# Expert products on gathered tokens: 23 tiles of one expert for two batches in place of 16 products for each batch

## The chip, the core and the metric

One core of one Trainium2 chip runs the whole program. The metric is the device time of one execution in microseconds (us). The engines are TensorE (PE; its weight loads stand as PEld), VectorE (DVE), ScalarE (ACT), GpSimd (POOL) and SyncE (SP, which only issues transfers). Each runs its own queue in order and waits on semaphores for the others.

## The reference

The input x has 8 batches of 512 tokens with 256 features. After a layer norm, two layers read the same normed x and both are added to x: a state-space layer (input product, 4-tap convolution, a linear recurrence, silu, output product), and attention with 16 heads plus a mixture of experts. The change touches the mixture only:

```python
gate = softmax(xn @ W_gate + b_gate)             # 8 experts
top_g, top_i = top_k(gate, 2)
combine = sum(one_hot(top_i, 8) * top_g[..., None], axis=2)
expert_out = einsum("bsd,edf->bsef", xn, W_experts) + b_experts
moe_out = einsum("bsef,bse->bsf", expert_out, combine)
out = x + state_space(xn) + attention(xn) + moe_out
```

Only two of the eight experts have a weight other than zero for a token.

## The kernel before

The program is a loop over steps, 256 of them and a tail of 16. Step t makes the scores of one block of queries for two heads on PE (`score`, tile SB), their row maximum on DVE (`largest`, mx, line 942), and, 11 steps behind, the turned scores (`turned`, TB), the exponentials on ACT (Pt, line 732) and the products with V (`values`). Eight steps are one group of heads, 32 steps one batch. SP copies the split q and k of a group into place (`half_stack`, 12 transfers each 8 steps) and the maxima (`max_row`).

Everything else is cut into units that a planner (`plan`) puts into the steps as PE has time by a table of costs: T (transposes of xn), V, Q (products), Z and Y (state space), O (its output product), C (transposed gate weights), P (attention turned back), X (maxima), and M, the expert products. A batch has 16 M units: i = 4 * (pair of experts) + (block of 128 tokens). Each is six matmuls of 512 columns, since every product is made of high and low halves (`three`, line 393): 128 tokens by two experts, for all tokens and all experts. ACT copies each half out of the bank times its gate weight into one of four buffers mt (line 595), POOL adds mt into acc, the output tile of the batch (`grow`, line 996). SP stores acc when all is in it (`store`) and loads x of a later batch into the same buffer.

The gates of a batch are computed in 22 small instructions on DVE, POOL and ACT (`gate`, tiles G, g4, cpad, cst). POOL besides that makes the low halves xl (line 1100) and yl (line 1108), which the Z and O units wait for, and adds attention (line 1005). At the start POOL also turns a kernel row into a matrix by three transfers that wait for each other (kd, rd, Rraw, lines 1080 to 1085); unit G of step 2 (line 485) waits for the last.

Of the kernel before, what the change touches and what calls it, by code (L numbers as in the profile page):

```python
# [7 lines left out]
F32R = mybir.dt.float32r  # L8
ALU = mybir.AluOpType
# [9 lines left out]
NM = 4  # L19
# [4 lines left out]

Unit = namedtuple("Unit", "kind b i t read bank use frees item before")

COST = {"T": 0.45, "V": 0.75, "Q": 1.42, "Z": 2.05, "Y": 1.42, "C": 0.45, "M": 1.42, "O": 1.5, "G": 2.8, "B": 0.55,
        "X": 0.15, "P": 0.45}

WANTED = {("T", i): -30 for i in range(2)}  # L30
WANTED.update({("V", i): -30 for i in range(4)})
WANTED.update({("Z", i): -20 for i in range(2)})
WANTED.update({("Q", i): -30 for i in range(4)})
WANTED.update({("Y", i): 4 * i - 8 for i in range(4)})
WANTED.update({("M", i): 2 * i for i in range(16)})
# [4 lines left out]
def plan():  # L40
# [6 lines left out]
    todo = [(k, b, i) for b in range(NB) for k, i in WANTED if b == 0 or k not in "GB"]  # L47
# [5 lines left out]
    def soonest(kind, b, i):  # L53

        if kind == "T":
            return max([ln.get(b, END) + 5, 7] + [after(("M", b - 2, n), 1) for n in range(16) if b >= 2])
# [10 lines left out]
        if kind == "Y":  # L67
            t = after(("Z", b, 1), 1) if i == 0 else after(("Y", b, i - 1), 4)
            return max(t, after(("B", 0, 3), 1)) if b == 0 else t
        if kind in "CM":  # L70
            return after(("V", b, 3), 8 if kind == "M" else 9)
# [7 lines left out]
    last, spent = STEPS + LAG - 3, 0.0  # L79
    for t in range(END):  # L80
        row = steps[t]
        left = sum(COST[u[0]] for u in todo) + sum(fixed(n) + (COST["X"] + COST["P"]) / 8 for n in range(t, last))
        spent = min(spent, 0.0) + left / max(last - t, 1) - fixed(t)
# [23 lines left out]
    for b in range(NB):  # L107
# [3 lines left out]
        assert b < 2 or at["M", b - 2, 15] < at["V", b, 3] + 6  # L111
# [4 lines left out]
    for t, row in steps.items():  # L116
        units[t] = []
        for k, (kind, b, i) in enumerate(row):
# [4 lines left out]
            frees[bank] += kind not in "MO"  # L123
# [5 lines left out]
            item += 2 * (kind in "MO")  # L129
# [16 lines left out]
ON = {name: on for name, on, _ in GATE}  # L146

# [19 lines left out]
def store_at(b):  # L167

    return max(UNIT["P", b, 4 * b + 3].read + 1, UNIT["M", b, 15].read + 2, UNIT["O", b, 3].read + 2)
# [13 lines left out]
def program(nc, x, wqk, bqk, wvg, bv, bg, win, bin_, cw, cwt, cb, A, AT_, Bp, Cp, Dp, wout, bout, wexp, bexp, out, kd, rd):  # L183
    ctx = ExitStack()
    with ctx:
# [18 lines left out]
        uc = sb("uc", [128, 2, 512])  # L204
# [6 lines left out]
        xTh1 = sb("xTh1", [128, 2, 512], F32R)  # L211
        xTl1 = sb("xTl1", [128, 2, 512], F32R)
        yh = sb("yh", [128, 4, 512], F32R)
        yl = sb("yl", [128, 4, 512], F32R)
        xTh = [sb("xTh0", [128, 2, 512], F32R), xTh1]
        xTl = [sb("xTl0", [128, 2, 512], F32R), xTl1]
# [43 lines left out]
        G = sb("G", [128, 6, 4, 8])  # L260
        g4 = sb("g4", [128, 6, 4])
        cpc = sb("cpc", [16, 1])
# [32 lines left out]
        s_out = sem("stored")  # L295
# [8 lines left out]
        s_ex, s_mh, s_ot = sem("exp_done"), sem("max_hi"), sem("ot_copied")  # L304
        s_xTh, s_V, s_qkh, s_zh = sem("xT_hi"), sem("V_copied"), sem("qk_hi"), sem("z_hi")
# [7 lines left out]
        s_cv, s_y, s_rc = sem("conv_taps"), sem("y_done"), sem("recip_done")  # L313
        s_kv, s_kp, s_Rl = sem("krylov_copied"), sem("kernel_row"), sem("R_lo")
        s_bw, s_bl = sem("bias_products"), sem("b_lo")

        s_id, s_pc, s_pad, s_rs = sem("identity"), sem("pool_consts"), sem("pads"), sem("rstd_done")
# [5 lines left out]
        def kp_rows(w):  # L323
# [10 lines left out]
            (uc[:, :, :].rearrange("p a c -> p (a c)").rearrange("p (k n) -> p k n", k=4), wout, wouth[:, :, :], woutl[:, :, :], 0.5),  # L334
# [19 lines left out]
        def bank_read(u):  # L354
            return (s_mc, u.item + 2) if u.kind in "MO" else (s_free[u.bank], u.frees)
# [9 lines left out]

        def x_loaded(b):
            return s_x[b % 3], 16 * (b // 3 if b % 3 == 0 else b // 3 + 1)

        def half_stack(e, g, h, s):

            r, p = g % 3, 64 * (g % 2) + 32 * h
# [857 lines left out]
```

## Time and profile before

| | |
|---|---|
| time, median of 3 runs | 831.44 us (830.02 to 836.89) |
| profiled execution, its own time | 838.47 us |
| its span, first to last instruction | 836.7 us |
| PE busy | 783.3 us, 94% |
| DVE busy | 579.1 us, 69% |
| ACT busy | 528.9 us, 63% |
| POOL busy | 380.3 us, 45% |

Busy time of PE is modelled and its matmuls overlap, so what a unit costs is read from the starts of its matmuls. Waiting, branching, register and transfer-issuing instructions are not in the busy times. A releaser after an idle time is inferred from the semaphores.

### The profile page before, as it was taken

Reading aid. Unit: us, or ns where it says so; the run is one execution under the profiler, and the core shown is the slowest. Engines: PE = TensorE matmul, PEld = TensorE weight load, DVE = VectorE, ACT = ScalarE, POOL = GpSimd, SP = SyncE. Lnnn points to the kernel's source line nnn. Section 1 sums busy time; section 2 is a strip of 40 time slices with the busy share of each in tenths; the row PEclk is TensorE's granted clock in tenths of the full one; section 3 lists DMA queues with packets and bytes.
Section 4 is the critical chain, followed back from the end, with each engine's and each line's share of the span. In section 5 each row is a group of like instructions: output and inputs, shape, how many; then the busy total and the mean of one; then the engine's idle time right before and its main releaser. Section 6 shows DMA issues by size and latency. Waiting matters only on the chain.

```text
span 836.7 us, 13124 instructions
## 1 busy us (share of the span) xinstructions
PE 783.3 (94%) x4366; PEld 449.9 (54%) x4366; DVE 579.1 (69%) x834; ACT 528.9 (63%) x916; POOL 380.3 (45%) x524
## 2 busy tenths in 40 slices
PE   7579998989999999999999999999899999999996
PEld 5445564545554555556555465555465555555552
DVE  4466885796648885688857877768866698557820
ACT  3324765667566775677756676667756677566674
POOL 4433463346253363524733527443454336354583
PEclk9868999999999999999999999999999999999997
DMA  5700111112011311112111311113101121112000
GB/s 191 179 8 17 26 39 39 40 38 74 17 43 36 89 39 39 40 39 81 32 34 29 83 38 39 40 39 90 40 19 39 30 57 38 40 40 64 2 2 26
DMA packets 32387, 39.69 MB, mean 47 GB/s; under 512 B 8433, under 2 KB 18455, under 8 KB 32320
## 3 DMA queue, kind: packets, MB, share of 16 engines
q1 hardware_dynamic: 31262, 36.94, 17.3%
q0 software_dynamic: 384, 1.12, 0.5%
q10 hardware_dynamic: 674, 0.80, 0.3%
q8 instruction: 35, 0.57, 0.3%
q14 instruction: 32, 0.26, 0.1%
HBM read 8.90 MB, written 4.59 MB: 16 GB/s over the span
## 4 chain that ended last, share of the span: by engine, by line
PE 70%; DVE 18%; issue 6%; POOL 2%; ACT 1%; DMA 1%; ACTq 0%; SPq 0%; POOLq 0%; DVEq 0%
PE PS L393 36%; PE SB L518 11%; DVE mx L942 9%; PE PS L548 9%; PE TB L532 5%; PE PS L443 4%; DVE ys L798 3%; PE PS L409 1%; DVE ys L794 1%; POOL acc L996 1%; PE PS L490 1%; PE PS L405 1%; DVE th L968 1%; DVE xl L830 1%; DMA kst<-qkh 1%
## 5 line engine op out<-in xcount | busy, mean ns | idle before, releaser
L942 DVE TENSOR_REDUCE mx<-SB 128x2 f32<-128x1024 f32 x256 | 312.9, 1222 | 188.0 <-PE SB L518 187.3
L996 POOL TENSOR_TENSOR acc<-acc,mt 128x256 f32<-128x256 f32 x320 | 248.3, 782 | 233.2 <-ACT mt L595 177.8
L732 ACT ACTIVATE Pt<-TB 128x1024 f32<-128x1024 f32 x256 | 262.8, 1027 | 33.5 <-PE TB L532 31.0
L595 ACT ACTIVATE mt<-PS,cpad 128x256 f32<-128x256 f32 x256 | 107.4, 471 | 93.7 <-PE PS L393 93.2
L518 PE MATMUL SB<-kst,qst 48*128 48x512 f32 x512 | 130.0, 504 | 26.2 <-DVE mx L942 19.4
L548 PE MATMUL PS<-Pt,V 128*17 128x512 f32 x1024 | 136.0, 603 | 1.1 <-ACT Pt L732 1.1
L518 PEld LDWEIGHTS SB<-kst,qst 48*128 48x128 f32 x512 | 48.3, 186 | 133.0 <-DVE mx L942 69.8
L393 PE MATMUL PS<-weh,xTh 128*128 128x512 f32 x256 | 112.9, 441 | 2.7 <-DVE ml L806 1.2
L532 PE MATMUL TB<-qst,kst 50*128 50x512 f32 x512 | 104.4, 403 | 1.6 <-ACT Pt L732 1.4
L393 PE MATMUL PS<-wel,xTh 128*128 128x512 f32 x256 | 101.8, 398 | 0.0
L393 PE MATMUL PS<-weh,xTl 128*128 128x512 f32 x256 | 101.4, 396 | 0.0
L798 DVE SCALAR_TENSOR_TENSOR ys<-uc,cwc,ys 128x511 f32<-128x511 f32 (+2 forms) x96 | 91.8, 957 | 0.1
L393 PEld LDWEIGHTS PS<-weh,xTh 128*128 128x128 f32 x256 | 49.2, 192 | 57.0 <-issue 31.2
L1005 POOL TENSOR_TENSOR acc<-acc,at 128x256 f32<-128x256 f32 x32 | 23.5, 734 | 84.6 <-DVE at L851 84.1
L1108 POOL TENSOR_TENSOR yl<-th,yh 128x512 fp32r<-128x512 f32 x32 | 42.9, 1340 | 27.1 <-ACT yh L673 27.1
L393 PEld LDWEIGHTS PS<-wel,xTh 128*128 128x128 f32 x256 | 48.5, 189 | 11.2
L393 PEld LDWEIGHTS PS<-weh,xTl 128*128 128x128 f32 x256 | 49.1, 192 | 6.3
L532 PEld LDWEIGHTS TB<-qst,kst 50*128 50x128 f32 x512 | 48.8, 187 | 6.7 <-ACT Pt L732 3.1
L626 ACT ACTIVATE qkh<-PS,bq 128x512 fp32r<-128x512 f32 x32 | 22.0, 688 | 33.3 <-PE PS L393 22.3
L548 PEld LDWEIGHTS PS<-Pt,V 128*17 128x17 f32 x1024 | 17.0, 95 | 47.3 <-issue 45.9
L637 ACT COPY uc<-PS 128x512 f32<-128x512 f32 x32 | 18.7, 586 | 31.4 <-PE PS L393 31.3
L393 PE MATMUL PS<-wouth,yh 128*128 128x256 f32 x128 | 38.0, 297 | 0.0
(147 smaller groups left out, 1148.5 us busy)
## 6 DMA issues: line engine op xcount, KB each, us to landing
qst<-qkh SPq DMA_DIRECT2D x126, 64.0 KB, 2.2
kst<-qkh SPq DMA_DIRECT2D x126, 64.0 KB, 2.2
out<-acc SPq DMA_DIRECT2D x8, 512.0 KB, 3.1
kst<-qkl SPq DMA_DIRECT2D x63, 64.0 KB, 2.2
qst<-qkl SPq DMA_DIRECT2D x63, 64.0 KB, 2.2
acc<-in_x SPq DMA_DIRECT2D x7, 512.0 KB, 4.2
Bt<-in_wexp SPq DMA_DIRECT2D x2, 512.0 KB, 6.9
raw<-in_wexp SPq DMA_DIRECT2D x2, 512.0 KB, 7.0
```

What stands on the lines that cost most here:

```text
L393: ins = e.matmul(P, u, v, start=(start and k == 0), stop=(stop and k == n - 1))
L443: ins = e.matmul(P[:, lo:lo + n], p[:, c, fs], q[:, r:r + n], start=(k == 0), stop=(k == 11))
L518: ins = e.matmul(SB[:, h, :], qst[rows, g % 3, jj, 128 * a:128 * a + 128], kst[rows, g % 3, jj, :], start=True, stop=True)
L532: ins = e.matmul(TB[:, h, :], kst[rows, g % 3, jj, 128 * a:128 * a + 128], qst[rows, g % 3, jj, :], start=True, stop=True)
L548: ins = e.matmul(OB[32 * j:32 * j + 17, :], V[:, g // 4 % 2, a, 4 * (g % 4) + j, :], Pt[:, (2 * m + j % 2) % NP, j // 2, :], start=(a == 0 ...
L595: return e.activation(mt[:, item % NM, :], P, ACT.Copy, scale=scale)
L732: e.activation(Pt[:, T % NP, :, :], TB[:, :, :], ACT.Exp, scale=0.25).then_inc(s_ex, 1)
L798: ins = e.scalar_tensor_tensor(out=y[:, s:512], in0=v[:, 0:512 - s], scalar=cwc[:, d, 3 - s:4 - s], in1=y[:, s:512], op0=ALU.mult, op1=ALU ...
L942: e.tensor_reduce(mx[:, g % 2, 0:2, 4 * jj + a], SB[:, :, :], AX.X, ALU.max).then_inc(s_mx, 1)
L996: e.tensor_tensor(v, v, mt[:, item % NM, :], ALU.add).then_inc(s_mt, 1)
L1005: e.tensor_tensor(v, v, at[:, :].rearrange("p (a c) -> p a c", a=4), ALU.add).then_inc(s_ad, 1)
L1108: e.tensor_tensor(yl[:, d, :], th[:, :], F(yh[:, d, :]), ALU.subtract).then_inc(s_yl, 1)
```

## The change

The 128 M units go. For each pair of batches (1024 tokens, 2048 choices) the choices are ranked by expert: unit R multiplies the 0/1 table of choices with a triangle of ones (9 small matmuls), and 13 small DVE instructions (`places`, `places_end`) make of it each choice's place in a list where every expert's part is padded to a multiple of 128, and the expert of each of 23 tiles. POOL scatters token number, output row and gate weight of each choice into that list in DRAM (16 indirect transfers of 128 rows of 16 bytes), SP writes the default list ahead of it and reads the finished one back. Then for each of the 23 tiles: POOL gathers 128 rows of 1 KB of xn from DRAM (`gather`, planned 3 steps ahead of unit E), unit E transposes them (two transposes of 128 columns), ACT and DVE make the high and low half, unit M multiplies them with the weights of that tile's expert (six matmuls of 256 columns, the columns' address in a register), ACT copies out times the gate weight (ysb, two buffers), and POOL adds the 128 rows into `out` in DRAM by an indirect transfer with an add. All 23 tiles are always computed.

The output is zeroed by SP in steps 9 to 16, and acc of a batch, which now gets only O and attention, is added to it by an adding transfer too. These 100 sums (92 tiles, 8 batches) form one chain: each waits until the one before has landed. ACT's copy of tile n waits for the sum of tile n-2. xn is also stored to DRAM by SP for each batch. SP's load of x for batch b waits for the sum of batch b-3.

By the planner of the changed kernel R stands in steps 17, 88, 152 and 216; the scatters follow from two steps later, two in each of eight steps, for the last pair four in each of four; the tiles' M units stand in steps 41 to 95, 106 to 159, 171 to 220 and 231 to 268, and their sums one or two steps later: 59 to 77 hold 12 sums (with that of batch 1), 124 to 142 hold 12, 187 to 215 hold 17, and 233 to 270 hold 25 (23 tiles and two batches). Steps 8 to 39 of before hold 16 M units, those of the change only two E units; before, 98 M units stand in steps 40 to 247 and 13 from 248 on; now 79 tiles and 13.

```diff
-NM = 4
+NM = 2
+NT = 23
 COST = {..., "C": 0.45,
-        "M": 1.42,
+        "R": 1.0, "E": 0.3, "M": 0.9,
...
+        if kind == "M":
+            return max([after(("E", b, i), 2)] + ([after(("M", b, i - 2), 3)] if i >= 2 else []))
...
 PE:
+                elif u.kind == "R":
+                    e.matmul(P[:, 0:72], upper[:, :], both[:, :, :].rearrange("p a c -> p (a c)"), start=True, stop=False)
+                    for a in range(8):
+                        ins = e.matmul(P[:, 8 * a + 8:72], ones[:, :],
+                                       both[:, a:a + 1, :].to_broadcast([128, 8 - a, 8]), start=False, stop=(a == 7))
+                elif u.kind == "E":
+                    e.wait_ge(s_xg[n % 3], 16 * (n // 3 + 1))
+                    for f in range(2):
+                        ins = e.transpose(P[:, 128 * f:128 * f + 128], xg[:, n % 3, 128 * f:128 * f + 128], ident[:, :])
                 elif u.kind == "M":
-                    ts, es = slice(128 * a, 128 * a + 128), slice(512 * e2, 512 * e2 + 512)
-                    ins = three(P[:, :], [((xTh[b % 2][:, f, ts], xTl[b % 2][:, f, ts]), (weh[:, f, es], wel[:, f, es]))
-                                          for f in range(2)])
+                    if i == 0:
+                        e.wait_ge(*placed(b // 2, "exi"))
+                        _, which[:] = nc.values_load_multi_w_load_instructions(exi[0:1, :], ...)
+                    cs = bass.ds(which[i], 256)
+                    ins = three(P[:, 0:256], [((xgh[:, n % 2, 128 * f:128 * f + 128], xgl[...]),
+                                               (weh[:, f, cs], wel[:, f, cs])) for f in range(2)])
...
 ACT:
                 elif u.kind == "M":
-                    for k in range(2):
-                        c = 2 * e2 + k
-                        mt_copy(u.item + k, P[:, 256 * k:256 * k + 256], cpad[:, b % 2, a, c:c + 1]).then_inc(s_mc, 1)
+                    if n >= 2:
+                        e.wait_ge(*summed(("M", n - 2)))
+                    e.activation(ysb[:, n % 2, :], P[:, 0:256], ACT.Copy,
+                                 scale=sid[:, b // 2 % 2, i, 2:3].bitcast(F32)).then_inc(s_free[u.bank], 1)
+                elif u.kind == "E":
+                    e.copy(xgh[:, n % 2, :], P[:, 0:256]).then_inc(s_xgh, 1)
...
 DVE:
+                elif u.kind == "E":
+                    ins = e.tensor_tensor(xgl[:, n % 2, :], P[:, 0:256], F(xgh[:, n % 2, :]), ALU.subtract)
...
 POOL:
-                if u.kind in "MO":
+                if u.kind == "O":
                     for k in range(2):
                         grow(...)
+            for k in range(8):
+                e.memset(k128[:, k:k + 1], 128.0 * k).then_inc(s_tri, 1)
+            for j in range(NT):
+                e.memset(nth[:, j:j + 1], float(j)).then_inc(s_tri, 1)
             e.wait_ge(s_kp, 2)
             e.dma_start(kd[:, 0:768], kp).then_inc(s_kd, 16)
...
+            def scatter(p, k):
+                e.wait_ge(*placed(p, "placei"))
+                for c in range(2):
+                    n = 2 * k + c
+                    e.indirect_dma_start(tab, bass.IndirectOffsetOnAxis(placei[:, n:n + 1], 0), idg[:, k, c, :],
+                                         None).then_inc(s_sc, 16)
+            def gather(n):
+                if n >= 3:
+                    e.wait_ge(*full("E", *TILES[n - 3]))
+                e.indirect_dma_start(xg[:, n % 3, :], None, xs[p],
+                                     bass.IndirectOffsetOnAxis(sid[:, p % 2, j, 0:1], 0)).then_inc(s_xg[n % 3], 16)
+            def add(what):
+                if SUMS[what] > 1:
+                    e.wait_ge(s_sum, 16 * SUMS[what] - 16)
+                if kind == "S":
+                    e.dma_start(out[k].rearrange("(a p) d -> p a d", p=128), acc[:, k % 3, :, :],
+                                accum_op=ALU.add).then_inc(s_sum, 16)
+                else:
+                    e.wait_ge(*freed("M", *TILES[k]))
+                    e.indirect_dma_start(out.rearrange("b t d -> (b t) d"),
+                                         bass.IndirectOffsetOnAxis(sid[:, k // NT % 2, k % NT, 1:2], 0),
+                                         ysb[:, k % 2, :], None, compute_op=ALU.add).then_inc(s_sum, 16)
...
 SP:
-                    if t == store_at(b):
-                        store(b)
+                    if b >= 3 and t == store_at(b - 3) + 2:
+                        e.wait_ge(*summed(("S", b - 3)))
+                        load_x(b)
+                    if t == ranked(p) + 3 + 8 // BLOCKS[p]:
+                        e.wait_ge(s_sc, 256 * (p + 1))
+                        e.dma_start(sid[:, p % 2, :, :], tab[...])
```

On PE, one expert unit before, with the scores of the next step behind it (weh and wel are the expert weights' halves, xTh and xTl the transposed tokens'):

```order
L393 MATMUL PS<-weh,xTh 128x512
L393 MATMUL PS<-weh,xTl 128x512
L393 MATMUL PS<-wel,xTh 128x512
L393 MATMUL PS<-weh,xTh 128x512
L393 MATMUL PS<-weh,xTl 128x512
L393 MATMUL PS<-wel,xTh 128x512
L518 MATMUL SB<-kst,qst 128x512 x2
```

The same engine in the changed kernel, one tile (M, then the next step's scores and the E unit of a later tile; ISA and REGISTER_ALU are instructions of PE's sequencer that compute or test the register):

```order
L481 ISA x3
L481 MATMUL PS<-weh,xgh 128x256
L481 ISA
L481 MATMUL PS<-weh,xgl 128x256
L481 ISA
L481 REGISTER_ALU
L481 MATMUL PS<-wel,xgh 128x256
L481 ISA x2
...
L627 MATMUL SB<-kst,qst 128x512 x2
L641 MATMUL TB<-qst,kst 128x512 x2
L558 MATMUL PS<-ident,xg 128x128 x2
```

Half the columns of each matmul are gone, two transposes have come, and 11 sequencer instructions of a tile (9 ISA, 2 REGISTER_ALU) now stand among its matmuls.

On POOL, the end of the program before (acc, at, mt, yl as above):

```order
L1108 TENSOR_TENSOR yl<-th,yh 128x512
L996 TENSOR_TENSOR acc<-acc,mt 128x256 x4
L1005 TENSOR_TENSOR acc<-acc,at 128x4x64
L996 TENSOR_TENSOR acc<-acc,mt 128x256 x10
L1005 TENSOR_TENSOR acc<-acc,at 128x4x64
```

And in the changed kernel (xg<-xs is a gather, out<-ysb the sum of a tile, out<-acc that of a batch):

```order
L1268 DMA xg<-xs,sid 128x256
L1183 TENSOR_TENSOR acc<-acc,at 128x4x64
L1268 DMA xg<-xs,sid 128x256
L1285 DMA out<-ysb,sid 4096x256 x2
L1268 DMA xg<-xs,sid 128x256
L1285 DMA out<-ysb,sid 4096x256 x3
L1183 TENSOR_TENSOR acc<-acc,at 128x4x64
L1285 DMA out<-ysb,sid 4096x256
L1281 DMA out<-acc 128x4x256
L1285 DMA out<-ysb,sid 4096x256
```

The adds of mt have left the queue; in their place stand transfers, each out<- one of which waits for the one above it to land.

## Rows read from the trace of the kernel before

**Rows 1.** The page: busy us (share of the span) and instructions of each engine.

```profile
PE 783.3 (94%) x4366; PEld 449.9 (54%) x4366; DVE 579.1 (69%) x834; ACT 528.9 (63%) x916; POOL 380.3 (45%) x524
```

**Rows 2.** By stretch: us; busy us (instructions) of PE, PEld, DVE, ACT, POOL; clock, DMA.

```profile
72.00:173.00 101.00, 94.93 (x525) 55.76 (x524) 76.76 (x109) 64.93 (x115) 48.52 (x63) 0.98 0.14 33
173.00:777.00 604.00, 582.25 (x3344) 331.23 (x3342) 443.88 (x623) 403.06 (x683) 271.50 (x371) 0.99 0.18 46
777.00:836.70 59.70, 51.23 (x282) 28.30 (x280) 22.74 (x28) 37.20 (x66) 32.99 (x40) 0.93 0.03 10
```

**Rows 3.** Timeline of DVE (start, us, instruction): the row maxima of steps 8, 40, 248.

```profile
72.08 1.23 DVE L942 TENSOR_REDUCE mx<-SB 128x2 f32<-128x1024 f32 x1 [3.05 <-PE SB L518]
...
172.94 1.21 DVE L942 TENSOR_REDUCE mx<-SB 128x2 f32<-128x1024 f32 x1
...
777.04 1.23 DVE L942 TENSOR_REDUCE mx<-SB 128x2 f32<-128x1024 f32 x1 [0.80 <-PE SB L518]
```

**Rows 4.** Groups: count, busy us, mean ns, then idle before and its releaser.

```profile
L996 POOL TENSOR_TENSOR acc<-acc,mt 128x256 f32<-128x256 f32 x320 | 248.3, 782 | 233.2 <-ACT mt L595 177.8
```

**Rows 5.** Timeline of PE: two M units back to back, then the next step.

```profile
804.97 0.50 PE L393 MATMUL PS<-weh,xTh 128*128 128x512 f32 x1
...
806.48 0.40 PE L393 MATMUL PS<-weh,xTh 128*128 128x512 f32 x1
...
807.63 0.39 PE L393 MATMUL PS<-wel,xTh 128*128 128x512 f32 x1
807.95 0.49 PE L532 MATMUL TB<-qst,kst 50*128 50x512 f32 x2
```

**Rows 6.** Timeline of PE: four transposes, then matmuls of 256 columns of an O unit.

```profile
811.38 0.66 PE L409 MATMUL PS<-ident,ot 128*128 128x128 f32 x4
811.80 0.36 PE L393 MATMUL PS<-wouth,yh 128*128 128x256 f32 x1
812.00 0.29 PE L393 MATMUL PS<-wouth,yl 128*128 128x256 f32 x1
...
813.20 0.28 PE L393 MATMUL PS<-woutl,yh 128*128 128x256 f32 x1
```

**Rows 7.** Groups of DVE by form: small instructions of the kind that comes.

```profile
L851 DVE TENSOR_TENSOR at<-PS,rc 128x256 f32<-128x256 f32 x32 | 13.6, 425 | 1.1
L876 DVE TENSOR_REDUCE g<-G 128x4 f32<-128x32 f32 x16 | 2.9, 180 | 0.4 <-POOL G L1020 0.2
```

**Rows 8.** Timeline of POOL at the start: memsets, and three transfers that wait for each other.

```profile
13.14 0.35 POOL L1075 MEMSET wr<- 128x1 f32 x8
...
26.32 0.51 POOL L1080 DMA_DIRECT2D kd<-ys  x1
31.56 0.55 POOL L1082 DMA_DIRECT2D rd<-kd  x1 [4.73 <-DMA kd<-ys]
36.38 0.57 POOL L1085 DMA_DIRECT2D ys<-rd  x1 [4.26 <-DMA rd<-kd]
```

**Rows 9.** Timeline of PE: unit G after its wait for the last of these.

```profile
43.94 4.43 PE L485 MATMUL PS<-ys,ot 128*1 128x512 f32 x8 [5.79 <-issue]
```

**Rows 10.** Sequencer gap of PE at a step's start (timeline of weight loads).

```profile
807.95 0.19 PEld L532 LDWEIGHTS TB<-qst,kst 50*128 50x128 f32 x2 [0.36 <-issue]
```

**Rows 11.** POOL groups that other engines wait for: xl and yl.

```profile
L1108 POOL TENSOR_TENSOR yl<-th,yh 128x512 fp32r<-128x512 f32 x32 | 42.9, 1340 | 27.1 <-ACT yh L673 27.1
L1100 POOL TENSOR_TENSOR xl<-xn,xh 128x256 fp32r<-128x256 f32 x32 | 24.7, 772 | 3.7 <-ACT xh L679 3.6
```

**Rows 12.** Transfers: issuing queue, count, KB each, median us from issue to landing.

```profile
out<-acc SPq DMA_DIRECT2D x8, 512.0 KB, 3.1
qst<-qkh POOLq DMA_DIRECT2D x2, 64.0 KB, 3.0
```

**Rows 13.** DVE groups by form: the convolution's taps, 511 and 509 columns.

```profile
L798 DVE SCALAR_TENSOR_TENSOR ys<-uc,cwc,ys 128x511 f32<-128x511 f32 x32 | 33.1, 1036 | 0.0
L798 DVE SCALAR_TENSOR_TENSOR ys<-uc,cwc,ys 128x509 f32<-128x509 f32 x32 | 25.9, 809 | 0.0
```

More of the change, by code:

```diff
@@ L146, with tile, ranked @@
 ON = {name: on for name, on, _ in GATE}
+TILES = [(2 * (n // NT) + 1, n % NT) for n in range(NTILES)]
+def tile(kind, n):
+    return UNIT[kind, *TILES[n]]
+def ranked(p):
+    return UNIT["R", 2 * p + 1, 0].read
 def gate_at(t, engine):
@@ L259, in program @@
         cwc = sb("cwc", [128, 4, 4])
-        G = sb("G", [128, 6, 4, 8])
+        G = sb("G", [128, 4, 4, 8])
         g4 = sb("g4", [128, 6, 4])
+        ysb = sb("ysb", [128, 2, 256])
+        upper = sb("upper", [128, 128])
+        ones = sb("ones", [128, 128])
+        pick = sb("pick", [128, 8, 2, 8])
+        both = sb("both", [128, 9, 8])
+        W1 = sb("W1", [128, 192])
+        W2 = sb("W2", [128, 8, 8])
+        cnt = sb("cnt", [128, 3, 8])
+        place = sb("place", [128, 8, 2])
+        placei = sb("placei", [128, 16], I32)
+        ex = sb("ex", [1, 2, NT])
+        exi = sb("exi", [1, NT], I32)
+        k128 = sb("k128", [128, 8])
+        lower = sb("lower", [128, 8, 8])
+        nth = sb("nth", [1, NT])
+        sid = sb("sid", [128, 2, NT, 4], I32)
+        idg = sb("idg", [128, 8, 2, 4], I32)
         cpc = sb("cpc", [16, 1])
@@ L367, in x_loaded, with placed, picks, gates @@
             return s_x[b % 3], 16 * (b // 3 if b % 3 == 0 else b // 3 + 1)
+        PLACES = ("more", "tiles", "prior", "first", "rank", "mine", "place", "placei", "end", "over", "expert", "last",
+                  "exi")
+        def placed(p, name):
+            return s_pos, len(PLACES) * p + PLACES.index(name) + 1
+        def picks(b, k):
+            return pick[:, 4 * (b % 2):4 * (b % 2) + 4, k, :]
+        def gates(b, k):
+            return idg[:, 4 * (b % 2):4 * (b % 2) + 4, k, 2].bitcast(F32)
+        def summed(what):
+            return s_sum, 16 * SUMS[what]
         def half_stack(e, g, h, s):
@@ L1102, in _ @@
                     split(W_E[t // 2 + 1])
+                for p in range(NPAIR):
+                    if t == max(ranked(p) - 8, 1):
+                        numbers(p)
+                    for k in range(8):
+                        if t == ranked(p) + 2 + k // BLOCKS[p]:
+                            scatter(p, k)
+                for n in range(NTILES):
+                    if t == tile("E", n).t - 3:
+                        gather(n)
+                for what in sums_at(t):
+                    add(what)
                 for b, d in y_read(t - 6):
                     e.wait_ge(s_yh, 4 * b + d + 1)
-                    if b == 0 and d < 2:
+                    if b == 0 and d == 0:
                         e.wait_ge(*full("B", 0, 3))
```

283 lines of the change are left out of this document (214 added, 69 removed).

## The prediction

> **What bounds the kernel now.** The page comes first: PE is busy 783 of 837 us, no other engine over 69% [rows 1]. The stretches say the same of each stage: from 173 to 777 us PE is busy 582 of 604 us, DVE 444, and the granted clock is 0.99, the upper of its two levels [rows 2]. The groups show who waits: POOL's adds stood 178 us for ACT's copies of expert products, which themselves follow PE [rows 4]. So a microsecond of matmuls taken off PE is a microsecond off the step, until the next engine is reached. The row maxima give the scale: steps 8 and 40 begin at 72.1 and 172.9 us, step 248 at 777.0 [rows 3], so 24 last steps take the last 60 us, 2.5 us each.
>
> **What goes off PE.** Two M units back to back took 2.98 us (804.97 to 807.95), 1.49 each; starts lie 0.23 us apart and the last is followed after 0.32, so a change of unit costs 0.09 [rows 5]. 128 of them: -191 us.
>
> **What comes on PE.** Matmuls of 256 columns start 0.12 us apart (ten from 812.00 to 813.20), transposes 0.105 (four from 811.38 to 811.80) [rows 6]. A tile is 6 x 0.12 + 0.09 = 0.81 for M and 2 x 0.105 + 0.09 = 0.30 for E; 92 tiles: +102. R: 36 small matmuls, at most 0.12 each: +4. Net -85 us.
>
> **Where DVE takes over.** From 72 to 173 us the kernel before has 16 M units, 24 us, and the change two E units. PE would fall from 95 to 71 busy us, but DVE has 76.8 there [rows 2], plus 13 instructions of R at 0.18 [rows 7]: 79. That stretch can't go below about 80; I take 83 and lose 6 of the 24: +6. Later DVE gets 79 of the 92 subtractions of E at 0.43 [rows 7] and the rest of R: 444 + 34 + 7 = 485. PE's 98 M units in these 208 steps become 79 tiles and three R: 604 - 146 + 88 + 3 = 549 us, 2.6 a step. DVE stays below PE, but at 88% a step's maxima are sooner late. Against this, 256 POOL adds leave; convolution taps of 511 and 509 columns differ by 1036 to 809 ns though their work is equal [rows 13], so something beside them holds them up. Bounds 0 and +14; I take +3.
>
> **The start.** 31 one-column memsets stand ahead of the first of POOL's three dependent transfers; eight take 0.35 us [rows 8]. Unit G waits for the last and PE stood 5.79 us for it [rows 9], so this goes to the end: +1.5.
>
> **PE's sequencer.** 11 register instructions stand in each tile and no row shows one. Below: 0, if they are through while the matmul ahead still runs. Above: one whole sequencer gap of 0.36 [rows 10] per tile, 34 us. They sit between matmuls of 0.12 us that the array has yet to run, so I lean to the low end: +6.
>
> **POOL.** It loses 256 adds of 0.78, 200 us [rows 4], and gets 248 indirect transfers. No row shows an indirect one; the plain ones over 128 rows took 0.55 and 0.57 us to issue [rows 8]. Below, that; above, twice it, because it reads 128 addresses as well; I take 1.0, in all 248 us. So POOL has time on the whole, and the question is what stands behind a long or waiting instruction in its queue: xl, which Z waits for, yl, which O waits for, the gates, and the gathers, which E waits for.
>
> The table scatters, 16 for each pair, fill 16 of the 20 us of eight steps, beside some 9 us of POOL's own (four xl, 3.1, two yl, 2.7 [rows 11], four adds, 3.1 [rows 4]). That is 5 us late, or some more with the sums between them, where xl or the first gathers of the pair come next, in about two of four pairs. SP waits in its queue for them too, with the next group's stacks behind. Bounds 0 (at 0.57 all fits) and 25; I take +10.
>
> SP's loads of x wait for a batch's sum, as they waited for its store before, which lands in 3.1 us [rows 12]; now that sum stands behind up to three others. max_row comes next in the queue, with three steps until PE needs it. Bounds 0 and 10; +3.
>
> **The chain of sums.** Its link, from one issue to the next, is what the total hangs on. Rows for it: POOL's transfers that wait for each other were issued 5.24 us (kd, 3 KB to DRAM) and 4.82 us (rd, 128 rows in DRAM) apart, in the busy start [rows 8]; SP's store of 512 KB lands in 3.1, POOL's copy inside the core in 3.0 [rows 12], the store with 0.57 of issue gives 3.7. An adding transfer reads its target as well. Below 3.7; above 6.0, the slower chain link plus a second 0.57 and some reading; I take 4.8, that of the 128-row transfer to DRAM, the nearest in kind. The anatomy of a GpSimd transfer in the Trainium skill's DMA: Bandwidth & Descriptors (section Anatomy of one DMA) gives about 2.0 us fixed plus bytes over 436 GB/s; with the issue that would be an estimated link of 2.9 us, and by it the chain binds nowhere. The trace's 4.82 and 5.24 disagree with it, in a stretch where other transfers were running.
>
> Middle pairs: 12 sums in steps 59 to 77 need 11 x 4.8 = 53 us and have 18 steps of 2.6, 47; the 17 of steps 187 to 215 need 77 and have 73. Being up to two steps (5 us) late is covered by the gathers' lead of three steps and by sparser steps behind; about 0 to 2. At 6.0 they need 66 and 96, which is 19 and 23 us over. Last pair: 25 sums are planned in steps 233 to 270, so 24 x 4.8 = 115 us in 37 x 2.5 = 92.5: +23. Nothing comes after to hide it. ACT's copy of tile n waits for sum n-2 with the exponentials behind it, so the loop itself slows. The program then ends on an added transfer with a second read instead of a store: +1.
>
> **Sum**, against the profile's own time, 838.5 (span 836.7 and 1.8 around it): 838.5 - 85 + 6 + 3 + 1.5 + 6 + 10 + 3 + 23 + 1 = 807. The profiled execution is 7.0 us above the median of the three runs, so the forecast is **800 us**, 4% faster.
>
> **Rivals.**
> *The sums are hidden.* If a link is 3.7 us, the last pair needs 89 us of its 92.5 and the 23 us are gone: 807 - 23 - 7 = 777. For it: landings of 3.1 us for a store of 512 KB and 3.0 for copies that POOL itself issued [rows 12]. Against: both dependent chains of POOL in the trace.
> *The sums become the bound, and the kernel is slower.* One mechanism, the link: at 6.0 us the last pair is 51.5 us over, and three dense stretches are over by 19, 19 and 23, of which 5 each is covered: 46. 807 - 23 + 51.5 + 46 - 7 = 874. It decides from about 5.3 us on: tail 35, middle 23, 807 - 23 + 58 - 7 = 835. For it: 5.24 was seen for a plain transfer of 3 KB, and the sums add addresses and an add. The Trainium skill speaks for it too: SBUF (SBUF: two separate sides) says that GpSimd and VectorE share a port pair that one of them holds for a whole instruction, and that descriptors written by GpSimd wait for it; the taps of 1036 against 809 ns agree that such instructions hold each other up [rows 13], and by that rule taps of 0.8 to 1.0 us would stand in front of some of the 100 links.
> *The smaller products don't pay on PE.* If each tile costs a whole sequencer gap, 34 us instead of 6: 807 + 28 - 7 = 828, no change. For it: 11 instructions beside 0.81 us of matmuls. Against: all but the first three stand behind a matmul of the same tile that is still running.
>
> **How the numbers follow.** Forecast 0.42, hidden sums 0.24, sums as the bound 0.22, sequencer 0.12. Within the forecast the small terms move by some 15 us, so a tenth of it ends within 1%. A measurement of this kernel can tell about 1% from no change. Faster: 0.42 x 0.9 + 0.24 = 0.62; the same: 0.04 + 0.12 = 0.16; slower: 0.22. The range reaches down past 777 to 766, small terms near their lower ends with hidden sums, and up to 860, a link of 5.75; of the outer cases about 0.15 is left out. The forecast's own range is 784 to 820.
>
> **What would show it.** Right: PE's busy time falls by some 85 us, DVE's rises to about 620, and in the last 40 steps POOL stands for out<-ysb at nearly each sum while ACT's ysb copies wait for the same transfer; sums are issued 4.5 to 5 us apart there. Wrong: sums 3.7 us apart with no wait (first rival), over 5.3 with ACT waiting in the middle pairs too (second), or matmuls of a tile starting more than 0.12 us apart with the gap put to issue (third). A wait of PE's E unit for gathers in most tiles would break the step that gave POOL's queue a mere 10 us.

## The result: 989 us where 800 were forecast, and the profile after

The changed kernel takes 989.18 us (median of 4 runs, 986.74 to 992.47), the kernel before beside it 834.16 (830.02 to 837.18): ratio 1.187, interval 1.179 to 1.194. The profiled execution took 986.94 us, its span is 985.2. First the page's busy times and its row of granted clock, which answer to [rows 1].

```profile
PE 786.0 (80%) x4406; PEld 456.5 (46%) x4406; DVE 610.4 (62%) x980; ACT 499.8 (51%) x844; POOL 508.3 (52%) x581
PEclk9777879977999898899999788777999898998975
```

PE has 85 us less work by the forecast's own prices, and yet its busy time rose from 783.3 to 786.0: at a lower granted clock the same matmuls take longer (mean 0.874, 0.970 before). PE stood for 985.2 - 786.0 = 199 us; before for 53. The same three stretches of steps as in [rows 2], cut at the row maxima of steps 8, 40 and 248 (columns as there):

```profile
67.30:176.80 109.50, 83.46 (x440) 46.57 (x440) 76.02 (x122) 52.85 (x81) 42.90 (x54) 0.83 0.33 75
176.80:906.50 729.70, 606.56 (x3491) 352.15 (x3490) 478.80 (x751) 391.89 (x659) 396.94 (x410) 0.89 0.39 71
906.50:985.20 78.70, 44.89 (x256) 24.51 (x254) 17.64 (x29) 30.80 (x52) 39.12 (x31) 0.78 0.36 53
```

All three are longer: 109.5 us for 101, 729.7 for 604, 78.7 for 59.7. No engine is full in any of them, so the time went into waits. PE's own, of after (what waited, for what: us in total, times, longest), then the one of before that answers to the first line:

```profile
PE SB L627 <- DVE mx L1115: 54.5, 48, 3.5
PE TB L641 <- ACT Pt L842: 25.7, 16, 3.7
PE PS L531 <- POOL xl L1347: 23.1, 5, 6.5
PE PS L558 <- DMA xg<-xs,sid: 21.8, 7, 5.8
```

```profile
PE SB L518 <- DVE mx L942: 19.4, 24, 2.1
```

Scores wait for row maxima, turned scores for exponentials, Z for xl and E for gathers. Before, only the first of these was there to speak of. The groups of the new transfers on POOL, and ACT's copy ysb (columns as in [rows 4]):

```profile
L1285 POOL DMA_INDIRECT out<-ysb,sid x92 | 150.4, 1634 | 138.9 <-DMA out<-ysb,sid 66.9 <-DMA out<-acc 37.9 <-ACT ysb L755 23.0
L1268 POOL DMA_INDIRECT xg<-xs,sid x92 | 95.5, 1038 | 30.3 <-issue 17.9 <-PE PS L558 8.6 <-DMA sid<-tab 2.2
L1257 POOL DMA_INDIRECT tab<-idg,placei x64 | 63.3, 989 | 18.7 <-issue 16.6 <-DVE cnt L1008 1.9 <-POOL acc L1183 0.2
L755 ACT ACTIVATE ysb<-PS,sid 128x256 f32<-128x256 f32 x92 | 43.7, 475 | 104.9 <-DMA out<-ysb,sid 70.3 <-PE PS L481 34.0 <-issue 0.5
```

### The profile page after: what moved, and what is told of

The parts are those of the page before. It is cut to its first block and busy times, and to the rows that moved or that the text cites. A ratio compares the mean times of both kernels' runs of the same rounds, so it can differ in the third digit from the quotient of the medians.

```text
span 985.2 us, 14512 instructions
## 1 busy us (share of the span) xinstructions
PE 786.0 (80%) x4406; PEld 456.5 (46%) x4406; DVE 610.4 (62%) x980; ACT 499.8 (51%) x844; POOL 508.3 (52%) x581
## 5 line engine op out<-in xcount | busy, mean ns | idle before, releaser
L1285 POOL DMA_INDIRECT out<-ysb,sid x92 | 150.4, 1634 | 138.9 <-DMA out<-ysb,sid 66.9
L1268 POOL DMA_INDIRECT xg<-xs,sid x92 | 95.5, 1038 | 30.3 <-issue 17.9
L755 ACT ACTIVATE ysb<-PS,sid 128x256 f32<-128x256 f32 x92 | 43.7, 475 | 104.9 <-DMA out<-ysb,sid 70.3
L1366 POOL TENSOR_TENSOR yl<-th,yh 128x512 fp32r<-128x512 f32 x32 | 47.8, 1492 | 71.0 <-ACT yh L783 70.7
L941 DVE TENSOR_TENSOR xgl<-PS,xgh 128x256 fp32r<-128x256 f32 x92 | 38.6, 420 | 68.3 <-ACT xgh L748 68.1
L1257 POOL DMA_INDIRECT tab<-idg,placei x64 | 63.3, 989 | 18.7 <-issue 16.6
L481 PE MATMUL PS<-weh,xgh 128*128 x184 | 67.5, 367 | 5.3 <-issue 2.5
L1174 POOL TENSOR_TENSOR acc<-acc,mt 128x256 f32<-128x256 f32 x64 | 56.9, 1062 | 13.1 <-ACT mt L702 12.9
L558 PE MATMUL PS<-ident,xg 128*128 128x128 f32 x184 | 39.3, 301 | 25.4 <-DMA xg<-xs,sid 21.8
L481 PE MATMUL PS<-wel,xgh 128*128 x184 | 57.5, 312 | 0.0
L481 PE MATMUL PS<-weh,xgl 128*128 x184 | 55.5, 301 | 0.0
```

What stands on the lines that cost most here:

```text
L481: ins = e.matmul(P, u, v, start=(start and k == 0), stop=(stop and k == n - 1))
L558: ins = e.transpose(P[:, 128 * f:128 * f + 128], xg[:, n % 3, 128 * f:128 * f + 128], ident[:, :])
L1174: e.tensor_tensor(v, v, mt[:, item % NM, :], ALU.add).then_inc(s_mt, 1)
L1257: e.indirect_dma_start(tab, bass.IndirectOffsetOnAxis(placei[:, n:n + 1], 0), idg[:, k, c, :], None).then_inc(s_sc, 16)
L1268: e.indirect_dma_start(xg[:, n % 3, :], None, xs[p], bass.IndirectOffsetOnAxis(sid[:, p % 2, j, 0:1], 0)).then_inc(s_xg[n % 3], 16)
L1285: e.indirect_dma_start(out.rearrange("b t d -> (b t) d"), bass.IndirectOffsetOnAxis(sid[:, k // NT % 2, k % NT, 1:2], 0), ysb[:, k % 2, :] ...
```

## The experiments

Unless said otherwise each is one run with a profile, beside a run of the kernel before on the same chip (830 to 839 us).

### Which of the new transfers costs what

Four kernels leave out transfers of the changed one, with the waits on them: the sums of tiles, the table scatters, the gathers but for three, and all of these. The eight batch sums stay in each.

```diff
 def sums_at(t):
-    return [("S", b) ...] + [("M", n) for n in range(NTILES) if tile("M", n).read + 1 == t]
+    return [("S", b) ...]
...
                         if t == ranked(p) + 2 + k // BLOCKS[p]:
-                            scatter(p, k)
+                            pass
...
-                for n in range(NTILES):
+                for n in range(3):
                     if t == tile("E", n).t - 3:
                         gather(n)
```

> The 92 tile sums are left out (the output lacks the experts' products); ranking, scatters, gathers, products and the eight batch sums stay. Theory chain: ACT's waits for sums (70 us) and POOL's (105 us) are the root, and the low clock follows from PE's waits, so about 870 us. Theory POOL time: any of the three kinds of indirect transfers costs by its time on POOL's queue, so about 930 (150 us of issue less). Theory PE: the tiles themselves are dear on PE, so no less than 970.

> The 64 scatters of places are left out, so that every tile takes default rows with weight zero; sums and gathers stay. Theory chain: only the two or three long waits for the low halves of the state space go, about 960 us. Theory POOL time: 63 us of issue and 19 of gaps, about 920. Theory PE: 980.

> All gathers but the first three are left out, the tiles multiply those rows again; scatters and sums stay. Theory chain: PE's waits for gathered rows go (25 us) and the link stays, about 950 us. Theory POOL time: 95 us of issue and 30 of gaps, about 900. Theory PE: 980.

> Tile sums, scatters and all but three gathers are left out; what is left is the ranking and all work of PE, ACT and DVE on 92 tiles. Theories chain and POOL time: 775 to 800 us, the prediction's sum without its terms for POOL, and a clock of 0.96 or more. Theory PE: above 880, because the tiles cost PE and DVE what they do in the changed kernel.

Measured: 893.5 us without sums (-96), 974.4 without scatters (-15), 945.9 without gathers (-43), 866.8 without any (-122). Sums are the dearest, as expected, but the fourth run decides: with all indirect transfers gone but three gathers the kernel is still 33 to 37 us slower than before (834.2, and 830.1 beside it), where the theories with the forecast's PE term had 775 to 800; theory PE, which had the tiles dear by themselves, wanted above 880 and missed too. So there are two errors, one in the transfers (122 us) and one in the part that was thought to gain.

### Is a microsecond off PE a microsecond off the step?

This is asked of the kernel before, alone, by cutting M units to one of their six matmuls (every second unit, then all):

```diff
+                    if i % 2 == 0:
+                        ins = e.matmul(P[:, :], xTh[b % 2][:, 0, ts], weh[:, 0, es], start=True, stop=True)
+                    else:
                         ins = three(P[:, :], [...])
```

> The kernel before, with 64 of its 128 M units (every second one) cut to one of their six matmuls, so part of the products isn't computed; all else stays, evictions and adds too. It takes 64 x 5 x 0.23 = 74 us of matmuls off PE. Theory PE (the step of the prediction): a microsecond off PE is a microsecond off the step, 830 - 74 = 756 us, clock as before (0.97). Theory loop: a step can't be shorter than score, row maximum and the way back to the next score (2.0 to 2.2 us, the shortest steps of before); 782 us by that floor alone, and some more if the granted clock falls while PE stands, so 780 to 805.

> As the run before, with all 128 M units cut to one of their six matmuls: 147 us of matmuls off PE. Theory PE: 830 - 147 = 683 us. Theory loop: the floor of 2.0 to 2.2 us takes most of the second half: 725 to 736 without a loss of clock, 750 to 790 with one, and the granted clock at 0.93 or less.

Measured: 809.4 us for 74 us of matmuls less, 787.9 for 147 less, beside 831.0. That is 0.29 us of time for each us off PE, both times; the second dose gave no less than the first. Theory PE is out; theory loop has the first run a little above its range (780 to 805) and the second inside. Page and longest wait of PE, with 74 us less and with 147 less:

```profile
PE 723.8 (90%) x4046; PEld 399.4 (49%) x4046; DVE 576.5 (71%) x834; ACT 526.4 (65%) x916; POOL 386.0 (48%) x524
PE SB L521 <- DVE mx L945: 43.5, 57, 2.9
```

```profile
PE 674.4 (86%) x3726; PEld 354.1 (45%) x3726; DVE 577.7 (73%) x834; ACT 522.9 (67%) x916; POOL 389.1 (50%) x524
PE SB L521 <- DVE mx L945: 70.7, 93, 3.0
```

PE's wait for the row maximum goes from 19.4 us in 24 places to 43.5 in 57 and 70.7 in 93. There is one score tile SB: the next score waits until DVE has read the last, and DVE waits for the score. PE's units fill the time in between; take them away and PE stands. Of the 147 us, PE's busy time fell by only 783.3 - 674.4 = 109, so 38 went into matmuls at a lower clock (mean 0.93 for 0.97); against the profiled run of before the span fell by 50.6, and the other 58 became idle time of PE.

The other side of the loop is DVE. In the kernel with all M units thin, 96 of the convolution's taps are cut to 63 columns and less:

```diff
-                    ins = e.scalar_tensor_tensor(out=y[:, s:512], in0=v[:, 0:512 - s], ..., in1=y[:, s:512], ...)
+                    ins = e.scalar_tensor_tensor(out=y[:, s:64], in0=v[:, 0:64 - s], ..., in1=y[:, s:64], ...)
```

> The kernel before with all M units cut to one matmul (787.9 us) and 96 of its 128 convolution taps on DVE cut from 509 to 511 columns to 61 to 63, so convolution and products are not computed in full: 70 to 75 us of DVE's work leave, nothing of PE's. Theory DVE in the loop: the row maximum stands behind other work of DVE and the next score behind the maximum, so a good part comes back: 730 to 765 us. Theory floor: score, maximum and the way back are the floor by themselves, 780 to 790 us.

Measured: 757.6 us, 30 less. DVE's busy time fell by 44 us and not by 70 to 75, for a tap of some 62 columns still took 455 ns on average. That average mixes two kinds, as the shortest, median and longest of each show (ns, first with whole taps, then with short ones):

```profile
L801 DVE SCALAR_TENSOR_TENSOR ys<-uc,cwc,ys 128x63 f32<-128x63 f32 (+2 forms) x96 | 43.6, 455 | 0.1
L801 DVE SCALAR_TENSOR_TENSOR ys<-uc,cwc,ys x96: 728/748/1760, 72.8 to 751.0; 128x511 f32<-128x511 f32 x32, 128x510 f32<-128x510 f32 x32, 128x509 f32<-128x509 f32 x32
L801 DVE SCALAR_TENSOR_TENSOR ys<-uc,cwc,ys x96: 260/278/1371, 70.8 to 723.3; 128x63 f32<-128x63 f32 x32, 128x62 f32<-128x62 f32 x32, 128x61 f32<-128x61 f32 x32
```

By the timelines, short taps with no instruction of POOL beside them took 0.26 to 0.28 us each and whole ones 0.73 to 0.74; only those beside one took longer.

So DVE, busy 73% of that kernel, gave 0.7 us for each us taken off it. PE's wait for the row maximum fell from 70.7 to 63.4 us, and its busy time by 18 us at a mean clock of 0.95 for 0.93. Theory DVE in the loop holds: PE and DVE take turns, and neither's busy share says how far one may be relieved alone.

### PE's sequencer, and matmuls put back

Two versions of the kernel without transfers: columns of the weights at fixed addresses, and on top of that M units of 512 columns, whose second half goes to waste.

```diff
-                    cs = bass.ds(which[i], 256)
+                    cs = slice(256 * (i // 3), 256 * (i // 3) + 256)
```

> The changed kernel without sums, table scatters and all but three gathers (866.8 us), and the columns of the weights at fixed addresses: no register loads and no address arithmetic on PE's sequencer. So expert and sums are not those of the reference. Theory sequencer: 92 tiles x 0.1 to 0.36 us come back, 832 to 857 us. Theory loop: the sequencer's work lies beside other waits, 862 to 868.

> As the run before, but each M unit of a tile multiplies 512 columns where it had 256, the second half going to waste: 92 x 6 x 0.11 = 61 us more matmuls for PE, nothing more for any other engine. Theory PE: the time rises by 61 us against the run before. Theory loop: the matmuls fill stretches in which PE stood, and the granted clock rises: plus 0 to 25 us against the run before, with the clock above 0.94.

Measured: 860.6 us for 866.8, so registers and addresses cost some 6 us, by one run each; that lies between the two theories and is what the forecast had. The wide units: 896.5, 36 more for 61 us of matmuls. That missed both expectations (61; 0 to 25). PE's busy time rose by only 49 us (736.7 to 786.1), at a clock of 0.941 instead of 0.931, and the span by 34.5, so 15 of the 49 filled waits. That is 0.59 us of time for each us put on PE: PE still decides in part of the steps. That in this plan it does so in more of them than in the kernel before (0.29) is inferred from the two rates.

### The wait at Z

In the kernel without transfers PE stands five times, 17.1 us, for xl, though POOL is busy 23% of it. The wait, then the timeline around step 52 (start, duration, engine, instruction, idle before), the rows in between left out:

```profile
PE PS L530 <- POOL xl L1341: 17.1, 5, 5.3
```

```profile
209.75 0.42 DVE L965 TENSOR_TENSOR at<-PS,rc 128x256 f32<-128x256 f32 x1
...
210.26 0.73 POOL L1177 TENSOR_TENSOR acc<-acc,at 128x256 f32<-128x256 f32 x1 [1.48 <-DVE at L965]
...
211.51 0.19 DVE L1043 TENSOR_TENSOR G<-G,idg 128x32 f32<-128x32 f32 x1
211.79 0.25 POOL L1197 TENSOR_TENSOR G<-G,wr 128x32 f32<-128x32 f32 x1 [0.80 <-DVE G L1043]
212.00 0.72 POOL L1341 TENSOR_TENSOR xl<-xn,xh 128x256 fp32r<-128x256 f32 x1
...
212.87 0.77 PE L530 MATMUL PS<-Rh,xh 128*128 128x512 f32 x1 [4.24 <-POOL xl L1341]
213.43 0.63 PE L530 MATMUL PS<-Rh,xl 128*128 128x512 f32 x1
213.85 0.63 PE L530 MATMUL PS<-Rl,xh 128*128 128x512 f32 x1
```

The last xl stands in POOL's queue behind an attention add and a gate operation, and these wait for DVE, which serves the units of the same step. The planner puts Z three steps behind the first xh (ACT's high half, of which xl is the rest), and here it came in the very step in which the fourth xl is made. The stretches before the wait, in it and behind it (columns as in [rows 2]):

```profile
204.00:208.60 4.60, 4.60 (x34) 2.51 (x32) 3.91 (x9) 3.94 (x8) 3.52 (x6) 1.00 0.44 106
208.60:212.80 4.20, 0.02 (x1) 0.00 (x0) 2.94 (x10) 0.85 (x3) 1.84 (x4) 0.97 0.27 65
212.80:215.90 3.10, 3.04 (x10) 2.79 (x11) 0.00 (x0) 0.00 (x0) 0.00 (x0) 0.50 0.00 0
215.90:218.40 2.50, 2.50 (x18) 2.22 (x17) 0.00 (x0) 0.00 (x0) 0.00 (x0) 0.98 0.00 0
```

PE works at the full clock, stands for 4.2 us, and then the granted clock is 0.50, its lower level, for 3.1 us, while DVE, ACT and POOL do nothing: Z's matmuls of 512 columns start 0.42 us apart (213.43 to 213.85), for 0.23 in [rows 5]. The Trainium skill describes this turn in TensorE: Matmul & The Clock Gate (HAM oscillation — how this bites in real kernels): in the kernel that it takes apart, each wait for a transfer lets the clock fall, and the next tile's matmuls start at the lower rate. These rows agree, for a wait of 4.2 us.

The edit against it, without transfers, in the whole changed kernel, without its sums, and as a control in the kernel before:

```diff
         if kind == "Z":
-            return max(xh[b] + 3, 4) if b in xh else END
+            return max(xh[b] + (6 if b else 3), 4) if b in xh else END
```

> The changed kernel without sums, table scatters and all but three gathers (866.8 us), with units Z planned at least six steps behind the first xh instead of three, so that POOL's xl are through when PE comes to them. Theory Z: PE's five waits there (17 us) and the half-clock matmuls behind them go, 835 to 852 us. Theory elsewhere: other waits take their place, 860 to 870 us.

> The changed kernel, whole, with units Z planned at least six steps behind the first xh instead of three, and nothing else edited (the planner moves other units by a few steps). Theory Z: the 45 us that the same edit gave without the indirect transfers come back here too, 935 to 955 us, and PE's wait for xl is nearly gone. Theory POOL: PE next stands for what comes behind sums in POOL's queue, gathers above all, so less than half of it comes back: 965 to 985 us.

> The changed kernel with Z six steps late as above and without the 92 sums of tiles (893.5 us with Z as planned). Theory Z: 845 to 860 us, so gathers and scatters cost 25 to 40 us over the 821.5 that stand without them. Theory POOL: scatters in front of xl and gathers kept PE waiting in any case, 870 to 893 us.

> The kernel before, whole, with Z planned six steps behind the first xh instead of three: the edit that gave 45 and 52 us in the changed kernel. Theory Z: it gave that because PE stood for xl behind other work of POOL; before, PE waits 0.2 us in all for xl, so the edit gives nothing, 824 to 840 us. Theory plan: any other order of the units near Z is better, and before gains as well: 800 to 822 us.

Measured: 821.5 us without transfers (-45, and more than expected), 937.6 for the whole kernel (-52), 865.2 without sums (-28, 5 above the range). The kernel before takes 834.9 with it, beside 837.2: nothing, and its PE had waited only 0.2 us for xl. So this is a cost of the changed plan: 17 us of waits, and with the slow clock and the steps behind it more. How much of the 45 is that isn't shown: by the row maxima some 25 us come back within ten steps of these five waits and 4 ahead of step 8, and the rest lies elsewhere, while the edit moves 160 of the 425 planned units, by up to 8 steps. PE's waits for xl are gone from the list of the whole kernel; that for exponentials, behind ACT's ysb copies, and that for the gathers stay:

```profile
PE TB L641 <- ACT Pt L842: 20.3, 14, 3.6
PE PS L558 <- DMA xg<-xs,sid: 11.5, 5, 4.1
```

The whole kernel with Z late is the fastest whole version with tiles, 937.6 us (one run), and still 12% slower than before.

### The sums: chain, ACT, POOL

One kernel splits the chain: tiles go by turns to two tensors in DRAM beside the output, so that a sum waits for the last but one. Another lets the sums read a constant tile, so that ACT's copy waits for none.

```diff
-                    e.indirect_dma_start(out.rearrange("b t d -> (b t) d"),
+                    e.indirect_dma_start(ysum[k % 2],
```

```diff
-                                         ysb[:, k % 2, :], None, compute_op=ALU.add).then_inc(s_sum, 16)
+                                         Bt[:, k % 4, 0:256], None, compute_op=ALU.add).then_inc(s_sum, 16)
```

> The changed kernel, but the sums of tiles go by turns into two tensors of their own in DRAM instead of the output, so each sum waits only for the last but one and for no batch sum; number, size and issue of the sums stay, and the output lacks the expert products. Theory chain (POOL stands 105 us for earlier sums, ACT's copies 70): most of the 95 us that the sums cost comes back, 915 to 945 us. Theory issue (1.63 us of POOL for each sum, 150 us in all, hold up what stands behind): 970 to 989 us.

> The changed kernel, but the sums read a constant tile, so ACT's copy into ysb waits for no sum; the chain on POOL stays as it is, and the values added are not the products. Theory ACT: the exponentials stood behind those copies (70 us of waits in 31 places) and PE behind the exponentials (25.7 us); 940 to 965 us. Theory POOL: what counts is what stands behind waiting sums in POOL's queue (xl, gathers); 975 to 990 us.

Measured: 951.2 us with three chains (-38), between the ranges of both theories, so the chain is at least some 40% of the 96 us; sums still wait for earlier ones there. With ACT free 990.2, no change: theory ACT falls for the kernel as planned. ACT's 70 us of waits went, and E's wait for gathers rose from 21.8 to 33.9 us and Z's for xl from 23.1 to 27.0; both come from POOL, so its queue is the likely cause, which these runs don't isolate.

### Tiles further apart

If the link (the time from one sum's issue to the next) is what binds, tiles two steps apart should cost less. Z is late here, the planner is asked for the tiles earlier, and gathers are issued five steps ahead; in a second version the gaps are two steps and one by turns, and gathers stay at three; the third is the first without scatters.

```diff
-            ... + [after(("E", b, i - 1), 0) if i else 0]
+            ... + [after(("E", b, i - 1), 2 * (b < NB - 1)) if i else 0]
```

> As the run before, with the tiles of the first three pairs planned at least two steps apart and their gathers, from each pair's fourth on, issued five steps ahead instead of three. Theory chain: at two steps (5.2 us) a link of 5.1 us fits, and POOL's and PE's waits for sums and gathers fall: 25 to 60 us below the run before. Theory issue: POOL's time for sums is what costs, and it stays: within 12 us of the run before.

> The changed kernel, whole, with Z six steps late (937.6 us) and the tiles of the first three pairs planned two steps and one step apart by turns, so that most are done before POOL issues the next pair's scatters; gathers three steps ahead as they were. Theory spacing: where tiles lay two steps apart in the last attempt (973.8 us), steps 56 to 95 took 116.7 us, as without any transfer, against 136.1; part of it comes here without the loss in the scatter stretches: 910 to 930 us. Theory issue: POOL's time is what costs however it is spread: 930 to 950 us.

> The kernel with Z late, tiles two steps apart and gathers five steps ahead (973.8 us), with the 64 table scatters left out, so the places gathered and added to are not the right ones. Theory scatters: 16 of them, 1.28 us apart, hold up a sum in POOL's queue, ACT's copy waits for the sum (11.1 us once) and the exponentials behind it (one step of 17.4 us); the four stretches of steps 96 to 103, 160 to 167 and 208 to 223 were 62 us longer than without transfers: 905 to 930 us. Theory order: scatters cost what they cost in the changed kernel, 15 us, and the loss is in the plan: 950 to 962 us.

Measured: 973.8 us, 36 more than with Z late alone, where one theory had 25 to 60 less and the other no change; 985.1 for the gentler version, above both its ranges; 925.9 without scatters. Steps 56 to 95 of the first did take 116.7 us, as with Z late and no transfers (117.8), for 136.1 with Z late alone. But the tiles pushed further back met the next pair's scatters, and step 98 took 17.4 us. POOL's timeline there, then ACT's and PE's:

```profile
355.62 1.60 POOL L1285 DMA_INDIRECT out<-ysb,sid  x1 [2.44 <-DMA out<-ysb,sid]
357.52 0.99 POOL L1257 DMA_INDIRECT tab<-idg,placei  x1 [0.30 <-issue]
358.82 0.98 POOL L1257 DMA_INDIRECT tab<-idg,placei  x1 [0.30 <-issue]
360.11 0.97 POOL L1257 DMA_INDIRECT tab<-idg,placei  x1 [0.30 <-issue]
361.38 0.97 POOL L1257 DMA_INDIRECT tab<-idg,placei  x1 [0.30 <-issue]
362.66 1.61 POOL L1285 DMA_INDIRECT out<-ysb,sid  x1 [0.30 <-issue]
```

```profile
355.44 0.47 ACT L755 ACTIVATE ysb<-PS,sid 128x256 f32<-128x256 f32 x1 [11.06 <-DMA out<-ysb,sid]
355.81 1.01 ACT L842 ACTIVATE Pt<-TB 128x1024 f32<-128x1024 f32 x1
```

```profile
356.88 0.80 PE L641 MATMUL TB<-qst,kst 50*128 50x512 f32 x2 [9.46 <-ACT Pt L842]
```

Scatters stand 1.28 us apart, 20.5 us for 16, and sums among them are late; ACT's copy stood 11.06 us for one, the exponentials behind it, and PE 9.46 us behind these. Here, unlike in the plan as it was, ACT's wait does stop the loop. Without scatters this version gains 48 us, inside theory scatters' range, so scatters and spacing work on each other. That the gentler version should be faster was wrong: ACT's waits for sums were 120 us in 36 places there, and which of its moved units did it isn't shown. So what the sums cost with Z late (937.6 - 865.2 = 72 us) isn't settled place by place: 17 lie behind the last row maximum (59.5 us to the end against 42.5 without sums), 55 in the steps, and no order of the units tried here removed them.

## Why the prediction was wrong, step by step

Measured from kernel to kernel, the 155 us are: all the new matmuls and evictions, Z late and the indirect transfers out, 821.5 - 834.2 = -13 (one run; -10 by the run of before beside it); Z and the other units where the plan has them, +45; the transfers, +122. By the forecast's terms the first was -85 + 6 + 3 + 1.5 + 6 = -68.5, the second not there, the third 10 + 3 + 23 + 1 = 37. So the three missed by some 56, 45 and 85 us. The first sign that the forecast named fails with them: PE's busy time was to fall by some 85 us, and it rose by 3.

**The step that failed first** is "So a microsecond of matmuls taken off PE is a microsecond off the step, until the next engine is reached". On the kernel before it is 0.29 us; 85 us are worth 25 by that rate, and less the forecast's 16.5 for what comes with them that is 8 or 9 off, near the 13 measured. PE's 94% [rows 1] was read as a bound of its own, while it was half of a loop of two engines over one tile: a step is score, maximum, next score, with units beside it. The next engine was looked for in the sums of busy time, and PE waits for it in single steps long before these are equal. In steps 8 to 39 the forecast took 83 us, from DVE's 79 busy us; without transfers they took 103.5, and 94.3 with Z late, for 100.9 before.

**The prices on PE were right.** A tile of after at full clock (PE's timeline; E, M, next unit):

```profile
751.31 0.44 PE L558 MATMUL PS<-ident,xg 128*128 128x128 f32 x2
751.51 0.37 PE L481 MATMUL PS<-weh,xgh 128*128 x1
751.71 0.28 PE L481 MATMUL PS<-weh,xgl 128*128 x1
751.83 0.28 PE L481 MATMUL PS<-wel,xgh 128*128 x1
751.95 0.28 PE L481 MATMUL PS<-weh,xgh 128*128 x1
752.07 0.28 PE L481 MATMUL PS<-weh,xgl 128*128 x1
752.19 0.28 PE L481 MATMUL PS<-wel,xgh 128*128 x1
752.31 0.38 PE L558 MATMUL PS<-ident,xg 128*128 128x128 f32 x2
```

M takes 0.80 us (0.81 forecast), E 0.20 (0.30), and the sequencer some 6 us in all (6). The forecast had no term for the clock: it took prices at the full level, and PE's standing lowered it.

**POOL's queue** was sized by issue time alone. 1.0 us was right for gathers (1.04) and scatters (0.99, 1.28 with the gap behind); a sum takes 1.63, so 309 us in all and not 248. The +10 for what stands behind the scatters, with nothing for the gathers, was far too small: the two cost 44 us with Z late (865.2 - 821.5). Yet the sign named for this, PE's E waiting in most tiles, didn't show: it waited in 7 of 92. And Z waits for xl even without transfers, in the timeline shown above because the new plan puts it into a full step; the rows of before couldn't show that, the order of both plans might have.

**The chain of sums.** POOL's timeline of the last sums of after:

```profile
956.92 1.57 POOL L1285 DMA_INDIRECT out<-ysb,sid  x1 [2.51 <-DMA out<-ysb,sid]
960.95 1.56 POOL L1285 DMA_INDIRECT out<-ysb,sid  x1 [2.46 <-DMA out<-ysb,sid]
963.35 0.72 POOL L1183 TENSOR_TENSOR acc<-acc,at 128x256 f32<-128x256 f32 x1 [0.85 <-DVE at L967]
964.97 1.56 POOL L1285 DMA_INDIRECT out<-ysb,sid  x1 [0.89 <-DMA out<-ysb,sid]
969.11 1.39 POOL L1281 DMA_DIRECT2D out<-acc  x1 [2.58 <-DMA out<-ysb,sid]
975.71 1.67 POOL L1285 DMA_INDIRECT out<-ysb,sid  x1 [5.21 <-DMA out<-acc]
```

A link of two tiles is 4.03 and 4.02 us here, between the 3.7 of the first rival and the 4.8 taken; in the whole kernel 39 sums waited for a tile's, at a median of 4.18. Behind a batch sum it is 6.60. The last pair's 25 sums went from 859.4 to 975.7, 116 us, where 115 were forecast. That the two agree is in part luck: only 15 of the 24 links waited for the sum before, most of them shorter than 4.8, and the other nine were held up by something else. With Z late the kernel's end lies 59.5 us behind the last row maximum, 36.7 without transfers: 23 us, the size forecast, of which 17 are the sums' (42.5 without them). The failed sentence is the one on the middle pairs, "about 0 to 2": the sums cost the steps some 55 us. That the cover of three steps was also eaten by scatters, gates and xl in the same queue is argued from the order of that queue and not shown place by place.

**The rivals.** The one that had the sign right, sums as the bound, rested on a link of over 5.3 us, and tile to tile that wasn't so (4.18); the forecast for it, 874, was 115 us too low, as it contained the failed -85. The taps that it set in front of the links cost them little: the 29 tile sums issued beside a tap took 1.70 us on average, the other 63 took 1.61. (At 5.3 us its dense stretches are over by 11, 11 and 12, which with 5 covered in each is 19 and not 23; and 92 gaps of 0.36 are 33 us and not 34. Neither changes a reading.) The rival that the smaller products don't pay gave the sequencer as its reason, and that is out (6 us); its headline was nearly right for another reason, the loop. No rival was that the loop can't use what PE saves, though PE's wait for mx, 19.4 us in 24 places, stood in the list of before.

## What to carry to other kernels

Where two engines hand one tile to and fro, a high busy share of one is no bound of its own: before a gain is booked, cut its work in the old kernel and see what comes back; here 0.29 of it did. A wait in front of TensorE can cost more than its length: behind the one of 4.2 us the granted clock was 0.50 for 3.1 us. A queue that is half idle can still be late at one place: look in the new order for what stands ahead of the instruction that the busiest engine waits for, in the same step.

## What the hardware showed that was not expected

Issuing an indirect transfer with an add held POOL for 1.63 us, one without for 0.99 to 1.04. An adding transfer of 512 KB released the next 6.60 us after its issue began, against 4.03 for 128 rows of 1 KB. A convolution tap on DVE cut from about 510 columns to about 62 went from 912 to 455 ns on average, but from 0.74 to 0.27 us where no instruction of POOL ran beside it; beside one, single taps took up to 1.76 us whole and 1.37 short. Gathers took 1.19 us to issue on average beside a tap and 0.99 without one.
